# P·V of a group of keys: one visit with 512 queries in place of two with 256

## The reference, cut to what matters

```python
q = (layernorm(x) @ W_q)      # 4 batches, 512 queries, 16 heads of 16
k, v = split(mem @ W_kv)      # 512 keys per batch
attn = softmax(einsum('bhqd,bhkd->bhqk', q, k) * SCALE)
out  = einsum('bhqk,bhkd->bhqd', attn, v)
x = x + tanh(g_xattn) * (out @ W_proj + b_proj)
x = x + tanh(g_ffn) * ffn(layernorm(x))   # router, 8 experts, top 2, and a shared expert
```

## Time and profile before

| | us |
|---|---|
| median of 3 runs | 604.12 (602.88 to 605.43) |
| span of the profiled execution | 619.1 |
| TensorE busy in it | 556.9 (90%) |
| VectorE busy | 308.5 (50%) |
| ScalarE busy | 237.2 (38%) |
| attention units, from the first score to the last visit | 90.7 to 316.7 |
| one unit in the middle of it | 13.2 |

### The profile page before, as it was taken

The page is one execution under the profiler, slowest core; times in us unless marked ns, Lnnn a source line. Parts: engine busy times, 40 slices in busy tenths (PEclk is TensorE's granted clock), DMA queues, the critical chain, the costliest instruction groups (busy, mean ns, idle before and its releaser), DMA issues.

```text
span 619.1 us, 9881 instructions
## 1 busy us (share of the span) xinstructions
PE 556.9 (90%) x2905; PEld 295.8 (48%) x2906; DVE 308.5 (50%) x611; ACT 237.2 (38%) x430; POOL 140.5 (23%) x169
## 2 busy tenths in 40 slices
PE   1899769999999999997999999299999999999992
PEld 1455212333333333333569455156666666666661
DVE  4465877777777777782563711022323323333320
ACT  1345216777667777773553200101221221221220
POOL 7063000110000010000000076400333333333332
PEclk9999758999999999997996899789999999999997
DMA  8147981663454465293000042212334334334322
GB/s 286 62 142 237 266 307 59 177 180 94 147 147 143 145 173 180 74 258 78 10 2 1 1 140 103 97 52 59 53 60 59 51 56 63 52 51 63 55 34 25
DMA packets 52646, 65.63 MB, mean 106 GB/s; under 512 B 6800, under 2 KB 44432, under 8 KB 52112
## 3 DMA queue, kind: packets, MB, share of 16 engines
q1 hardware_dynamic: 33440, 39.84, 22.2%
q0 software_dynamic: 7152, 9.34, 9.5%
q10 hardware_dynamic: 12032, 16.17, 8.5%
HBM read 37.93 MB, written 27.20 MB: 105 GB/s over the span
## 4 chain that ended last, share of the span: by engine, by line
PE 70%; DVE 7%; SPq 6%; another core or an unknown queue 5%; DMA 4%; issue 4%; ACT 2%; ACTq 1%; POOLq 0%; POOL 0%; DVEq 0%
PE ps L886 54%; PE ps L958 9%; DVE neg_max L676 3%; SPq L295 2%; SPq L285 2%; PE ps L1174 2%; DMA unit_region<-nm_parts 2%; DVE slot_rows L625 2%; PE ps L1153 1%; DMA gates<-in_g_ffn 1%; PE ps L967 1%; PE ps L1070 1%; PE ps L897 1%; DVE dn_region L648 1%
## 5 line engine op out<-in xcount | busy, mean ns | idle before, releaser
L676 DVE TENSOR_REDUCE neg_max<-ps 128x2 f32<-128x1024 f32 x128 | 155.8, 1223 | 45.6 <-PE ps L886 45.6
L517 ACT ACTIVATE ctx_region<-ps 128x512 f32<-128x512 f32 x256 | 144.6, 595 | 79.5 <-PE ps L886 77.5
L886 PE MATMUL ps<-unit_region 96*128 96x512 bf16 (+1 forms) x512 | 152.6, 403 | 12.3 <-DMA unit_region<-nm_parts 5.8
L886 PE MATMUL ps<-up_region,unit_region 128*128 x312 | 110.8, 498 | 2.3 <-issue 0.6
L441 POOL DMA_INDIRECT out<-unit_region x39 | 60.6, 1553 | 155.7 <-DVE unit_region L855 130.3
L886 PE MATMUL ps<-dn_region,unit_region 128*128 (+1 forms) x330 | 81.7, 391 | 13.4 <-DVE unit_region L754 12.8
L886 PEld LDWEIGHTS ps<-unit_region 96*128 96x128 bf16 (+1 forms) x512 | 40.3, 99 | 98.9 <-ACT ctx_region L517 52.1
L958 PE MATMUL ps<-ctx_region,unit_region 128*32 128x256 f32 x1024 | 82.2, 394 | 0.1
L886 PEld LDWEIGHTS ps<-dn_region,unit_region 128*128 128x128 f32 x330 | 64.5, 197 | 33.1 <-issue 14.4
L886 PEld LDWEIGHTS ps<-up_region,unit_region 128*128 128x128 f32 x312 | 56.1, 189 | 40.0 <-issue 6.8
L847 DVE TENSOR_TENSOR unit_region<-unit_region,ps 128x384 f32<-128x384 f32 x39 | 21.6, 555 | 84.4 <-PE ps L886 75.2
(11 more groups left out here) (119 smaller groups left out, 455.1 us busy)
## 6 DMA issues: line engine op xcount, KB each, us to landing
up_region<-in_w_upT ACTq DMA_DIRECT2D x9, 768.0 KB, 4.3
qk_parts<-up_region SPq DMA_DIRECT2D x32, 192.0 KB, 3.7
unit_region<-qk_parts SPq DMA_DIRECT2D x32, 192.0 KB, 3.0
x_slots<-empty ACTq DMA_DIRECT2D x1, 5031.0 KB, 20.6
unit_region<-x_slots SPq DMA_DIRECT2D x39, 129.0 KB
v_rows<-dn_region SPq DMA_DIRECT2D x4, 1024.0 KB, 5.9
unit_region<-qk_parts SPq DMA_DIRECT2D x32, 128.0 KB, 3.0
unit_region<-v_rows SPq DMA_DIRECT2D x16, 256.0 KB, 3.6
```

The costliest lines, as they stand in the source:

```text
L517: nc.scalar.activation(probs[:, k % 8, :], bank(4 + k % 2), ACT.Exp).then_inc(exp_done, 1)
L676: nc.vector.tensor_reduce(neg_max[:, s, 2 * p:2 * p + 2], bank(2 * (p % 2), 2), AX.X, ALU.max, negate=True).then_inc(max_done, 1)
L886: return nc.tensor.matmul(o_, w, m, start=start, stop=stop)
```

## The change

`pv` loses its argument `half`. One call now covers all 512 queries, and the calls in `slot` stand at every fourth step in place of every second.

```diff
-            def pv(u, s, kt, half, first=False):
-
-                if half == 0:
-                    pe.wait_ge(exp_done, u * TB * HG + kt * HG + HG)
-                    if kt == 0 and not first:
-                        pe.wait_ge(o_done, u)
-                cols = slice(half * T // 2, (half + 1) * T // 2)
+            def pv(u, s, kt, first=False):
+                pe.wait_ge(exp_done, u * TB * HG + kt * HG + HG)
+                if kt == 0 and not first:
+                    pe.wait_ge(o_done, u)
                 for h in range(HG):
-
-                    last = nc.tensor.matmul(bank(6)[h * VW:(h + 1) * VW, cols], v_unit[:, s, kt, h * VW:(h + 1) * VW],
-                                            probs[:, (kt * HG + h) % 8, cols], start=kt == 0 and half == 0,
-                                            stop=kt == TB - 1, skip_group_check=True)
-                if half == 1:
-                    last.then_inc(pv_done, 1)
+                    last = nc.tensor.matmul(bank(6)[h * VW:(h + 1) * VW, :], v_unit[:, s, kt, h * VW:(h + 1) * VW],
+                                            probs[:, (kt * HG + h) % 8, :], start=kt == 0, stop=kt == TB - 1,
+                                            skip_group_check=True)
+                last.then_inc(pv_done, 1)
...
-                    if k in (2, 3) and not first:
-                        pv(u - 1, (r - 1) % NG, TB - 1, k - 2)
+                    if k == 2 and not first:
+                        pv(u - 1, (r - 1) % NG, TB - 1)
...
-                    if kt >= 1 and k % 2 == 1:
-                        pv(u, s, kt - 1, k % HG // 2, first)
+                    if kt >= 1 and k % HG == 1:
+                        pv(u, s, kt - 1, first)
...
-            for half in range(2):
-                pv(UNITS - 1, (UNITS - 1) % NG, TB - 1, half)
+            pv(UNITS - 1, (UNITS - 1) % NG, TB - 1)
```

## The result

The changed kernel takes 608.0 us (median of 4 runs, 605.69 to 608.96), the kernel before on the same chip 603.7 us. The ratio is 1.0069, with a 95% interval of 1.0044 to 1.0094: the change makes the kernel 4.3 us slower. The forecast was 606.0 us, in a range of 601 to 609.5, with 0.66 on "no change" and 0.21 on "slower".

A forecast was written before the change was run, and what follows sets the result against it. TensorE's instruction sequence was taken to bound the attention. With +0.1 us up to slot 14 and +1.8 us in slots 14 and 15, +1.9 us on 604.12 gave 606.0 us, with an 8-in-10 range of 601 to 609.5.

The forecast's parts named there:

- What bounds the kernel: In mid-attention a unit lasts as long as TensorE's instructions take one behind the other, 13.23 us.
- the sum: All terms together: +0.1 us up to slot 14 and +1.8 us in slots 14 and 15, giving +1.9 us.
- The price of a joined visit: A wide visit adds 1.09 us against 2 x 0.66 for two narrow ones, saving 0.23 us of TensorE per pair.
- the bounds: Cheapest wide visits take at most 2.5 us off; dearer ones add some 2; together 603 to 609 us.
- The waits that eat it: Behind a visit, scores three and four wait for exponentials, so the 0.23 us saved are paid again.
- -1.0 us for the nine slots 2 to 4, 6 to 8 and 10 to 12: Bursts there change by +0.13, -0.08 and -0.16 us, together -0.11 us per unit.
- Slot 14's late start, +0.3: Slot 14 still waits for the maxima's DMA when slot 13 is faster; with ScalarE's later exponentials, +0.3 us.
- Slots 14 and 15, +1.8 us: No maximum tiles fill bursts: new waits for copies, exponentials and the last exponential cost 3.6 us, joined pairs save 1.8.
- Slots 0 and 1, +0.4: The same wait as at loop-round starts, with no turns in slot 0 to fill it: +0.4 us for both.
- Rival 1: Attention waits don't appear: all 14.5 us kept, 589.6 us, or 597.8 with half the waits; chance 0.13.
- Rival 2, the clock: New waits in slot 14 keep TensorE's clock low for longer, +2.9 us, 608.9 us; chance 0.12.
- The transfer to the timed median: The difference from the 619.1 us profile is put on the timed median of 604.12 us, giving 606.0 us.

The follow-up runs named there:

- dma_moved: Changed kernel with ScalarE's two expert-weight DMAs issued behind exponentials 9 and 13 of a slot; 617.6 us, ratio to before 0.9998.
- the first pair: The profiles on record of the kernel before and the changed kernel, no edit; attention 225.9 and 229.4 us.
- tail_narrow: Changed kernel with narrow visits at their old places in slots 14 and 15, the very last visit still wide; 620.5 us, ratio to before 1.0019.
- the second pair: Second profiles of the kernel before and the changed kernel, no edit; attention 225.2 and 228.4 us, changed kernel's timed ratio 0.9999.
- spread: Changed kernel with maximum tiles moved between second and third score behind a visit, and the turn of maxima behind score 3; 616.9 us, ratio to before 0.9975.
- combo_late: Changed kernel with moved maximum tiles, moved DMA issues, narrow visits in slots 14 and 15, and x_slots cleared behind slot 15; 608.6 us, ratio to before 0.9856.
- the combination: Changed kernel with moved maximum tiles, moved DMA issues, and narrow visits in slots 14 and 15; 613.4 us, ratio to before 0.9897.
- clear_late_before: Kernel before with the clearing of x_slots issued behind slot 15 in place of ahead of slot 13; 612.3 us, ratio to before 0.9867.

## Why the prediction was right, and where it was off

- **The outcome as a whole:** right in direction and inside the range, but 608.0 us is near its upper end. The favoured outcome, no change within 0.5%, isn't what the first measurement shows (0.69% slower, interval from 0.44), and of the 4.3 us measured the sum had 1.9. The width of the range covered a term that was missing, the DMA issues below.
- **What bounds the kernel:** right in the main. Short exponentials left the unit of before at 13.23 us. But this isn't TensorE's work alone: 0.25 us of the unit was a wait of the turn of maxima for VectorE, which isn't in the list of rows 3.
- **The price of a joined visit:** right. Entry 0.31, passes 0.45 and 0.55 were forecast and measured, and short exponentials brought 0.59 us of saving per unit out, with VectorE keeping most of the rest. In the bounds there is a slip: passes of 0.43 and 0.215 + 0.33 take 0.025 off a burst and not 0.04, so 1.6 us off the sum and not 2.5. Nothing hangs on it, since the passes came out as assumed.
- **The waits that eat it:** right. Scores behind a visit were forecast at 0, 0.45, 1.08 and 1.57, and are at 0, 0.45, 1.08 and 1.57 (210.98 to 212.54). A unit without DMA issues is 13.13 us (forecast 13.12), 0.10 less than before, and its three stretches, forecast at 4.07, 5.89 and 3.16, measure 4.05, 5.92 and 3.16 in slot 8. The list has 4.8 us of waits for exponentials where some 10 were forecast; as said, it leaves out those behind a running matmul.
- **"-1.0 us for the nine slots 2 to 4, 6 to 8 and 10 to 12": this is the step that failed.** I took the two DMA issues of ScalarE for a matter of loop starts. Three slots of every four have them. Before the change they were hidden in the six that don't start a round, since a visit stood between steps 15 and 0 and gave ScalarE time; without it score 2 waits. Six slots are 0.22 us longer (13.49 to 13.27) where I had 0.11 shorter, together +2.0 us. Only slots 4, 8 and 12 gained (-0.10 each). The slots at a round's start were forecast at +0.19 and measured at +0.20 and +0.22. dma_moved shows the cause: with the issues under the wide visits nearly all units are 13.13.
- **Slot 14's late start, +0.3:** from the turn in slot 13 to that in slot 14 it is +0.5 us in the first pair of profiles and +0.2 in the second.
- **Slots 14 and 15, +1.8 us:** right in kind and size in the first pair, +2.1 us (33.5 to 35.6 from the turn of maxima), and 1.7 to 2.5 by tail_narrow. In the second pair it is +1.2, because the changed kernel's profile has 3.4 us at 1.2 GHz there and the other three 6.8. The last visit waited 0.76 us as worked out, and `project` in three places.
- **Slots 0 and 1, +0.4:** not seen by itself. In the profiles on record it was -0.6, because the clock rose 3.8 us after the first score in place of 5.9; in the second pair it was +0.5.
- **The sum:** with the missing term it is +3.9 us, against +4.3 timed and +3.4 and +3.2 in the two pairs of profiles. That it comes so near is in part chance: single terms differ by up to 1.1 us between the pairs, with the place and length of the pieces at 1.2 GHz.
- **Rival 1:** its reason against itself held. What the prediction reads from rows 4 and 8 for it stands in rows 4 only (the last pass starts at 209.68, the next score at 210.01); rows 8 show no visit.
- **Rival 2, the clock:** it didn't happen in the changed kernel; the piece at 1.2 GHz behind the DMA wait was 6.8 us in both profiles on record. At slot 0 such a piece did get longer in three other runs: it lasted until 9.0 us after the first score in spread, 8.8 in the changed kernel with short exponentials and 8.0 in combo_late, against 5.9 before. No run shows why.
- **The transfer to the timed median:** the difference could be carried over, but I had not noticed that the profile of before holds some 15 us in a later stage. Its timed runs, near 604 us, can hardly have had them, though none of these was profiled.

## What to carry to other kernels

When work on the bounding engine is gathered in larger pieces, look at what its partner does during the piece. Here TensorE could be no more than two scores ahead, so a lump twice as long left ScalarE idle and made TensorE wait afterwards for what that idle time would have covered; the time saved in switching came back as waits. Gathering paid here when the work between the lumps was put into another order too (a unit of 12.72 us), until the next engine, VectorE, set the pace. More score banks would be another way, not tried here. And count for each slot everything that the partner's queue has to do there, DMA issues too: two issues of 0.6 us that had been hidden cost 0.35 us a slot once the slack was gone. And don't take a short list of waits for proof that one engine sets the pace: look whether each instruction starts right after what it waits for has ended. The 0.25 us of VectorE in a unit before were in no list, and the list of the combination pointed elsewhere.

## What the runs showed of the hardware

- Sets of four float32 matmuls side by side in four strips of 32 columns follow on each other without a gap that the trace shows, also from one visit to the next (0.215 us per pass of 256 columns). The change between them and bfloat16 matmuls over the array's 128 columns costs 0.09 us in (0.31 for 0.22) and 0.12 out (0.33 for 0.215).
- Two DMA issues between activations hold ScalarE for 0.6 us each: the next exponential starts 1.30 us after the one before it, in place of 0.49 (slot 7 of the changed kernel).
- In the twelve profiles with a wait of 2.8 to 4.5 us for the maxima's DMA ahead of slot 14 the granted clock fell to 1.2 GHz there, for 3.4 or 6.8 us. In the two without it (clear_late_before, combo_late) it stayed at 2.4 GHz to the attention's end.
- Exponentials of 512 columns that follow on each other start 0.49 us apart and last 0.60. The Trainium skill, "ScalarE: Activation LUTs", section What ACT_TABLE_LOAD costs, says that back-to-back activations overlap by about 93 ns; the trace agrees, with an overlap of 0.10 us (0.60 less 0.49, before rounding).
- The shared-expert stage, the same in all kernels here, took 59.9 us in one profile and 66 to 79 us in the others. In the second profile of before, ScalarE's activations there wait up to 20.7 us for something that the trace gives only as `remote`. What it is stays open.
